# Constants and weights loaded inside the first attention's own programs, first batch first

## The reference

```
q_in  = x + pos_enc ;  kv_in = ctx + pos_enc
q     = layer_norm(q_in) @ Wq ;  k, v = layer_norm(kv_in) @ Wk, Wv
y     = layer_norm(q_in) + softmax(q k^T / sqrt(8)) v @ Wo
y     = y + gelu(layer_norm(y) @ W1 + b1) @ W2 + b2
```

## Time and profile before

| | us |
|---|---|
| median of 3 runs | 2394.16 (2392.81 to 2394.26) |
| profiled execution, its own time | 2392.34 |
| its span in the trace | 2390.6 |
| PE busy | 2199.2 (92%) |
| DVE busy | 1464.7 (61%) |
| ACT busy | 1314.9 (55%) |
| POOL busy | 697.8 (29%) |

### The profile page before, as it was taken

One profiled execution on the slowest core, in us unless ns is written; L12 is line 12 of the kernel. 1 busy time (PEld: TensorE's weight loads), 2 busy tenths in 40 slices (PEclk: granted clock), 3 DMA queues, 4 the chain that ended last, 5 costly groups with the idle time before them and its releaser, 6 DMA issues. The chain is left out here.

```text
span 2390.6 us, 49371 instructions
## 1 busy us (share of the span) xinstructions
PE 2199.2 (92%) x18720; PEld 1815.7 (76%) x18720; DVE 1464.7 (61%) x2824; ACT 1314.9 (55%) x3809; POOL 697.8 (29%) x664
## 2 busy tenths in 40 slices
PE   5999978999878799999999999999998889999979
PEld 3666646877767688888888888888886776776668
DVE  4788743444463566666666666666666337999953
ACT  3777743454543454444445544444444439999953
POOL 4443302101170533020111503030101406677740
PEclk9999988999989899999999999999999899999989
DMA  3000001000010101010100001010000210000000
GB/s 123 20 15 11 2 1 54 2 2 2 2 36 22 61 17 45 1 36 10 30 16 10 28 19 36 3 34 1 1 1 36 71 50 7 2 2 2 2 9 28
DMA packets 33671, 50.70 MB, mean 21 GB/s; under 512 B 2592, under 2 KB 22048, under 8 KB 32416
## 3 DMA queue, kind: packets, MB, share of 16 engines
q1 hardware_dynamic: 33440, 47.53, 6.4%
HBM read 45.43 MB, written 2.10 MB: 20 GB/s over the span
## 5 line engine op out<-in xcount | busy, mean ns | idle before, releaser
L605 ACT ACTIVATE l_probs<-l_s_psum,l_neg_max 128x129 f32<-128x129 f32 x512 | 181.5, 367 | 266.6 <-DVE l_neg_max L656 266.6
L678 DVE TENSOR_TENSOR x<-x,l_o_psum 128x512 f32<-128x512 f32 x256 | 176.0, 688 | 187.7 <-PE l_o_psum L559 186.1
L2310 ACT ACTIVATE l_probs<-l_probs,l_neg_max 128x128 f32<-128x128 f32 x512 | 210.7, 531 | 0.0
L445 POOL TENSOR_TENSOR l_head_w_high<-l_head_raw,one 128x768 fp32r<-128x768 f32 x32 | 47.2, 1476 | 516.1 <-PE l_o_psum L559 516.0
L590 ACT ACTIVATE l_KT<-l_k_psum,cols 128x512 f32<-128x512 f32 x128 | 88.2, 689 | 198.5 <-PE l_k_psum L122 198.5
L1159 DVE TENSOR_REDUCE l_neg_max<-l_psum 128x2 f32<-128x512 f32 x256 | 164.7, 683 | 47.6 <-PE l_psum L955 47.5
L2141 POOL TENSOR_TENSOR l_probs<-l_probs,l_mask_add 128x512 f32<-128x512 f32 x128 | 162.1, 1288 | 85.1 <-DVE l_probs L2367 85.1
L559 PE MATMUL l_o_psum<-l_head_w_high,l_context_low 128*128 128x256 f32 x512 | 155.5, 304 | 8.6 <-DVE l_context_low L661 8.6
L1094 ACT ACTIVATE l_PT<-l_psum 128x512 f32<-128x512 f32 x256 | 132.1, 603 | 55.3 <-PE l_psum L983 52.7
L661 DVE SCALAR_TENSOR_TENSOR l_context_low<-l_c_psum,cols,l_context_high 128x512 fp32r<-128x512 f32 x128 | 95.8, 749 | 106.2 <-ACT l_context_high L597 105.4
L1666 DVE TENSOR_REDUCE l_neg_max<-l_psum 128x2 f32<-128x512 f32 x128 | 84.7, 687 | 117.7 <-PE l_psum L1480 117.7
(11 more groups left out here) (279 smaller groups left out, 6650.0 us busy)
## 6 DMA issues: line engine op xcount, KB each, us to landing
l_head_raw<-in_l_heads SPq DMA_DIRECT2D x32, 384.0 KB, 3.0
l_w<-in_l_w SPq DMA_DIRECT2D x4, 1024.0 KB, 8.4
l_ctx_in<-in_ctx_T SPq DMA_DIRECT2D x16, 256.0 KB, 5.3
l_value_raw<-in_l_values SPq DMA_DIRECT2D x8, 512.0 KB, 3.5
l_value_rows<-in_l_rows SPq DMA_DIRECT2D x8, 512.0 KB, 5.1
l_x_in<-in_x_T SPq DMA_DIRECT2D x16, 128.0 KB, 2.2
l_x_in<-in_ctx_T SPq DMA_DIRECT2D x16, 128.0 KB, 2.5
values<-in_l_w SPq DMA_DIRECT2D x2, 1024.0 KB, 5.9
```

The lines of the kernel that those rows point to most:

```text
L605: last = act.activation(probs[:, i, :], scores[:, i // 2, i % 2, :], ACT.Exp, bias=neg_max[:, i:i + 1], scale=1.0, accum_out=den[:, i:i + 1])
L678: dve.tensor_tensor(out=x, in0=x, in1=o_bank[:, :], op=ALU.add).then_inc(o_free, 1)
L2310: last = act.activation(p, p, ACT.Exp, bias=neg_max[:, s % SCORES3, m:m + 1], scale=1.0, accum_out=den[:, u % 2, 4 * r + m:4 * r + m + 1])
```

## The change

`load_constants` and its Block are gone. Its memsets, selects and the cast become `make_constants`, called at the head of POOL's program in `attention0`. The DMAs move into SP's program there, in a new order: load(0), pos, shapes, cols, load(1), the four attention weights, load(2), load(3), the two feed-forward weights, rows, layer 1's six weights, then load(4) and on; at its end SP waits for the feed-forward weights and rows. Each group has a semaphore of its own. POOL waits for shapes and then for pos ahead of place(0), ACT waits for cols, PE waits for the constants and the attention weights. The memsets of neg_parts and V move from POOL to DVE; ACT no longer waits for them.

```diff
-def load_constants(c):
-
-    nc = c.nc
-    loaded, made, shapes_loaded = (c.lasting(n) for n in ("constants_loaded", "constants_made", "shapes_loaded"))
-    with nc.Block() as block:
-
-        @block.sync
-        def _(sync):
-            sync.dma_start(c.shapes[:, :], c.dram["shapes"]).then_inc(shapes_loaded, 16)
-            sync.dma_start(c.cols[:, :], c.dram["cols"]).then_inc(loaded, 16)
-            sync.dma_start(c.rows[:, :], c.dram["rows"].rearrange("(a n) -> a n", a=1).to_broadcast([P, N_ROWS]))\
-                .then_inc(loaded, 16)
-            mine = [n for n in WEIGHTS_01 if n.startswith("l0")]
-            for name in mine:
-                sync.dma_start(c.w[name][:, :, :], c.dram[name]).then_inc(loaded, 16)
-            sync.dma_start(c.pos[:, :, :], c.dram["pos"]).then_inc(loaded, 16)
-            sync.wait_ge(loaded, 16 * (3 + len(mine)))
...
-            pool.wait_ge(made, 11)
+L0_ATTENTION = ("l0_wq", "l0_wk", "l0_wv", "l0_wo")
+
+
+def make_constants(pool, c):
+
+    pool.memset(c.ident[:, :], 0.0).then_inc(c.made, 1)
...
+    pool.wait_ge(c.shapes_loaded, 16)
+    pool.tensor_copy(c.select[:, :], c.shapes[:, 2 * H:3 * H + 8]).then_inc(c.made, 1)
...
-            for u in range(B):
+            load(0)
+            sync.dma_start(c.pos[:, :, :], c.dram["pos"]).then_inc(c.pos_loaded, 16)
+            sync.dma_start(c.shapes[:, :], c.dram["shapes"]).then_inc(c.shapes_loaded, 16)
+            sync.dma_start(c.cols[:, :], c.dram["cols"]).then_inc(c.cols_loaded, 16)
+            load(1)
+            load_weights(sync, c, L0_ATTENTION, c.l0_loaded)
+            load(2)
+            load(3)
+            load_weights(sync, c, ("l0_w1", "l0_w2"), c.rest_loaded)
+            sync.dma_start(c.rows[:, :], c.dram["rows"].rearrange("(a n) -> a n", a=1).to_broadcast([P, N_ROWS]))\
+                .then_inc(c.rest_loaded, 16)
+            load_weights(sync, c, LAYER1_WEIGHTS, c.l1_loaded)
+            for u in range(4, B):
                 load(u)
-                if u == 3:
-                    load_weights(sync, c, LAYER1_WEIGHTS, c.l1_loaded)
+            sync.wait_ge(c.rest_loaded, 16 * 3)
...
-            pool.memset(neg_parts[:, :, :], 0.0).then_inc(set_up, 1)
-            pool.memset(V[:, :, :, :, :], 0.0).then_inc(set_up, 1)
-            pool.wait_ge(set_up, 2)
-            pool.memset(V[:, :, :, :, 8:9], 1.0).then_inc(set_up, 1)
+            make_constants(pool, c)
+            pool.wait_ge(c.pos_loaded, 16)
...
         def _(pe):
+            pe.wait_ge(c.made, 11)
+            pe.wait_ge(c.l0_loaded, 16 * len(L0_ATTENTION))
             pe.wait_ge(set_up, 3)
...
         def _(act):
-            act.wait_ge(set_up, 3)
+            act.wait_ge(c.cols_loaded, 16)
...
         def _(dve):
+            dve.memset(neg_parts[:, :, :], 0.0).then_inc(set_up, 1)
+            dve.memset(V[:, :, :, :, :], 0.0).then_inc(set_up, 1)
+            dve.wait_ge(set_up, 2)
+            dve.memset(V[:, :, :, :, 8:9], 1.0).then_inc(set_up, 1)
             dve.wait_ge(set_up, 3)
```

More of the change, by code:

```diff
@@ new lines @@
+L0_ATTENTION = ("l0_wq", "l0_wk", "l0_wv", "l0_wo")
+def make_constants(pool, c):
+    pool.memset(c.ident[:, :], 0.0).then_inc(c.made, 1)
+    pool.memset(c.ident_bf[:, :], 0.0).then_inc(c.made, 1)
+    pool.memset(c.ones_bf[:, :], 1.0).then_inc(c.made, 1)
+    pool.memset(c.minus_half[:, :], -0.5).then_inc(c.made, 1)
+    pool.memset(c.epsilons[:, 0:1], 1e-5).then_inc(c.made, 1)
+    pool.memset(c.epsilons[:, 1:2], 1e-6).then_inc(c.made, 1)
+    pool.memset(c.quarter[:, :], 0.25).then_inc(c.made, 1)
+    pool.memset(c.one[:, :], 1.0).then_inc(c.made, 1)
+    pool.wait_ge(c.made, 8)
+    for m in (c.ident, c.ident_bf):
+        pool.affine_select(out=m[:, :], in_=m[:, :], compare_op=ALU.not_equal, fill=1.0, base=0,
+                           pattern=[[-1, P]], channel_multiplier=1).then_inc(c.made, 1)
+    pool.wait_ge(c.shapes_loaded, 16)
+    pool.tensor_copy(c.select[:, :], c.shapes[:, 2 * H:3 * H + 8]).then_inc(c.made, 1)
@@ L2471, in build @@
         c.lasting = lambda n: ctx.enter_context(nc.semaphore(n))
+        c.made, c.pos_loaded, c.shapes_loaded = (c.lasting(n) for n in ("constants_made", "pos_loaded", "shapes_loaded"))
+        c.cols_loaded, c.l0_loaded, c.rest_loaded = (c.lasting(n) for n in ("cols_loaded", "l0_loaded", "rest_loaded"))
         c.l1_loaded = c.lasting("l1_weights_loaded")
@@ L2507, in build @@
                         c.pos = pos
-                        load_constants(c)
                         attention0(c)
```

## The result

The changed kernel takes 2387.94 us (median of 13 runs, 2383.06 to 2391.86), the kernel before 2394.06 in the same series (13 runs, 2391.49 to 2403.72). The ratio estimated from all these runs is 0.9971, with a 95% interval of 0.9961 to 0.9981: 6.9 us faster, between 4.5 and 9.3 (the two medians alone differ by 6.1). A second series gave 0.9976 (0.9964 to 0.9988). The forecast was 2384.0 with 9.4 us of gain; the median lies in the range of 2380.5 to 2388.5, close to its upper end, and the gain is about three quarters of the forecast.

The account below looks back on a forecast made before the run. PE was busy 92% of the span, so the gain had to come from the start-up chain ahead of its first matmul: 9.4 us earlier, all later terms nothing. Forecast 2384.0 us, between 2382.9 and 2384.8; range 2380.5 to 2388.5.

Parts of the forecast that it names:

- place(0) and its three conditions: At start-up, place(0) needs x and context, pos, and shapes with its cast; forecast at 5.1 us (4.6 to 7.3), before 14.47.
- 3.1 us for pos: At start-up, the transfer time assumed for pos with 256 KB ahead of it, landing it at 4.75 us.
- 543 KB by bytes: Start-up check: x, context, pos and shapes total 543 KB, there at 4.4 us, or 4.8 with completion.
- rival 1: At start-up, pos takes 5.4 us and place(0) begins at 7.3; gain 7.2, time 2386.9; chance 0.09.
- What is late next: Inputs after place(0): load(1) at most 0.3 us late; load(2), attention weights and others cost nothing.
- load(4): At place(4) on POOL: lands at 26.6 us, 2.8 late, but round(1) at 32.2 leaves 4.3 us; price nothing.
- Rival 3: At place(4) on POOL, load(4) lands after 30.9 us (237 GB/s), stalling the pipeline; 2394.6 us at 165 GB/s; chance 0.04.
- DVE's new memsets: At DVE's start: memsets end at 3.0 us, or 5.3 at double price, before DVE is wanted at 6.4; cost nothing.
- `attention0` and each later stage then end 9.4 earlier with the same lengths.: From `attention0` to the end: the start-up lead of 9.4 us is kept through every stage.
- the prediction's own last sign: In the stages after start-up: the prediction is wrong if a later stage has another length than before.
- Rival 2: PE's clock rises later in some stretches, losing 2.6 to 5 us, time 2389 to 2391, or gives 2.6 back; chance 0.07.
- The sum: Whole kernel: 2392.34 less 9.4 gives 2382.9, the median less 9.4 gives 2384.8; 2384.0 taken between.

Follow-up runs that it names:

- b3: The changed kernel with two more transfers of 1024 KB queued behind layer 1's weights and ahead of load(4); ratio 0.9958 (0.9943 to 0.9973).
- c2: The kernel before with only the memsets of neg_parts and V moved from POOL to DVE; ratio 1.0012 (1.0003 to 1.0021).
- a4: The changed kernel with POOL's round waiting, from batch 2 on, for DVE's subtraction of the batch before; 2385.23 us, ratio 0.9971 (0.9960 to 0.9983).
- c3: The changed kernel with eight more one-column memsets at the start of DVE's program; ratio 0.9968 (0.9958 to 0.9977).
- a3: The kernel before with POOL's round waiting, from batch 2 on, for DVE's subtraction of the batch before; ratio 1.0002 (0.9993 to 1.0011).
- b2: The changed kernel with a Block and its barrier kept for POOL's fills, without DMAs; ratio 0.9969 (0.9956 to 0.9981).
- b1: The changed kernel with the transfers in the old order, so only the barrier is gone; ratio 0.9998 (0.9985 to 1.0012).
- b4: a4 with ACT's table load moved ahead of its wait for cols; 2383.92 us, ratio 0.9952 (0.9933 to 0.9970).
- c4: b4 with the wait of POOL's round from batch 1 on instead of batch 2; 2384.36 us, ratio 0.9954 (0.9941 to 0.9968).
- c1: The changed kernel with the memsets of neg_parts and V back on POOL, behind the constants; ratio 0.9971 (0.9962 to 0.9981).

## Why the prediction was right, and where it was off

- **place(0) and its three conditions.** Forecast 5.1, measured 5.20, and shapes came last as said. The 3.1 us for pos and the 543 KB by bytes were good prices. That pos could take the 5.4 of its old row was rival 1; it didn't happen in any of the kernels with the new order.
- **What is late next.** load(1) was 0.29 us late at POOL, and root(0) began 2.77 after place(0) in place of 2.73. The attention weights and cols waited for nobody. PE began at 13.11 (forecast 12.9).
- **load(4).** Forecast 26.6 and round(1) at 32.2 released by ACT with 4.3 us left; measured 26.11, 31.50 and 4.11. The flat rate of 282 GB/s was luck in part: in the changed kernel the stream moved 203 to 238 GB/s from 4 to 10 us and 421 to 438 from 16 to 22, and only the mean from 4 us to the landing, 6.37 MB in 22.1 us or 288 GB/s, is about the one assumed. That everything issued ahead lands ahead, which the count of bytes takes for granted, agrees with the kernel before: the first 64 KB weight, issued at 2.10 after the 1408 KB of rows at 1.63, took 6.3 us and landed at 8.4, rows at 8.1.

```profile
rows<-in_rows SPq DMA_DIRECT2D x1, 1408.0 KB, 6.5
```

  load(4) was issued at 13.49 and not at 12.8, since SP's issue of wo took 1.37 us in place of 0.43; it landed 12 us later, behind what the queue held, so this cost nothing. Its decisive point is where the sum put it (place(4) near 31), by b3. Rival 3 needed 237 GB/s or less and didn't happen.
- **"DVE's new memsets ... Nothing."** This is the step that failed. As work they are hidden, as the sum said: they end at 3.4 and DVE is wanted at 6.6. But each instruction added at the head of DVE's program moves all later ones, and with them the place where an instruction is issued 0.17 us late. In this kernel that place fell on a pair where DVE and POOL start within 0.01 us. The price read from the trace is 1.0 us for each of two lost races. c2 has the move of the memsets alone, with one race lost, and is slower than before by 2.9 us (0.7 to 5.0).
- **"`attention0` and each later stage then end 9.4 earlier with the same lengths."** By the prediction's own last sign this is a miss: the body of `attention0` is 2.8 us longer (245.2 against 242.4), 3.4 in the second profile. Two of these are the races. The bodies of the eight traces without a lost race differ by 0.9 among themselves (241.5 to 242.4). The rest goes with a fall of the granted clock ahead of the stage's end: in the stretch 320 to 324 us of the changed kernel it reads 0.79, where the kernel before has 1.00.

```profile
320.00:324.00 4.00, 2.21 (x26) 1.07 (x26) 0.00 (x0) 2.34 (x5) 0.00 (x0) 0.79 0.00 0
```

  This fall, of 3 us, is in five of the six traces with a lost race and in none of the eight without. Why it goes with the races stays open.
- **Rival 2, the clock.** The form was right and the size too small in one place. I priced the stretches after `attention0` (0.9 us each). The larger effect is in the first batches: with the rise of the clock within 2 us of exp0, exp0 to nT0 takes 52.0 to 52.1 us; 5 or more later it takes 53.2 to 56.0. It can be worth 4 us, and it differs between runs of one kernel. From nT15 to the end the 14 traces have 2045.8 to 2052.6 us, and show no relation to the change. The three runs at hand, within 1.5 us, made me think too little of it: the 13 of the kernel before in the result lie within 12.
- **The sum.** In the two profiled executions: 9.3 at the start, 0.8 more in the first batches through the clock, less 2.8 in the body, gives 7.3 at nT15; 1.0 more goes in the stages behind, whose lengths differ as much between runs of one kernel, and 6.3 are left in the span. The ratio gives 6.9. The mechanism of the start-up was right, and the term that was missing in the traces is the 2 us of the races, with what goes along with them. The times of the runs don't resolve that term: a4 and c3, without a lost race, gain 6.9 us (4.1 to 9.6) and 7.7 (5.5 to 10.1), the changed kernel 6.9 (4.5 to 9.3). What else keeps the runs below 9.4 stays open.
- **The range.** That the median lies in it is luck in part. Its upper end was put there for a late place(0) (rival 1), which didn't happen; the median is 0.6 us inside it, and six of the 13 runs lie above it.

## What to carry to other kernels

A start-up chain can be priced from the timeline to some tenths of a microsecond: order of issue, time per issue, bytes ahead in the queue, and what each engine waits for last; most of the lead at place(0) came from the order of the transfers (7.5 us) and little from the barrier (1.8). A steady pipeline in which VectorE and GpSimd are released at the same moment and one blocks the other, as here, is fragile: an edit far away, on an idle engine, cost a microsecond per collision in this trace, so it is worth looking for ties, and a wait that orders the pair was free here (a3: ratio 1.0002). Where runs scatter by 3 us and more, compare lengths between the same two instructions in the traces, and keep the stretches at another clock apart.

## What the runs showed of the hardware

**A late issue at a fixed place of a program.** With DVE's program as in the changed kernel, the subtraction of batch 9 is issued 0.39 us after the cast and elsewhere 0.22. With two instructions more (b2) the delay comes ahead of the cast, whose idle time reads 0.58 in place of 0.23; with eight more (c3) it is off the pair. In the 2 us from 196 on the DMA view of the changed kernel has one packet of kind "instruction" on queue 14. It moves with the late instruction: in all nine traces in which one of the pair is late at batch 9, such a packet starts 0.66 to 0.69 us after the start of the late subtraction, or 0.57 to 0.59 after that of the late cast, and in c3 it starts 3.1 us ahead of the cast. That the delay has to do with the fetch of DVE's instructions is likely from this; no run shows that the fetch causes it. The Trainium skill, page "Advanced Engine Details and Errata", section "ISA Cache", says that instructions are cached in large lines, of which an engine holds only two; a delay at a fixed place would fit, and no run here measures the cache.

**The second lost race has another cause.** At batch 12 the subtraction isn't late after the cast (0.22), the cast itself comes 0.03 us later than in other batches, and 0.03 is enough. In b1 it is less still: the subtraction starts 0.006 us after the round and is blocked, while in batches in which it starts up to 0.004 after the round it isn't. The delay is there in a4, b4 and c4 too, whose wait keeps it from costing a race. The lost race is gone with DVE's old program (c1), with eight more instructions (c3) and in both kernels with a Block ahead (b2, c2). What makes the 0.03 wasn't found.

**PE's clock at the start.** In the changed kernel's first profile the granted clock is 0.50 from 22 to 39 us, that is 1.2 GHz, after it had been 1.00 for 3 us:

```profile
22.00:24.00 2.00, 1.99 (x10) 1.59 (x8) 2.00 (x5) 2.00 (x6) 2.00 (x2) 0.50 1.03 325
36.00:38.00 2.00, 2.00 (x25) 1.42 (x18) 0.04 (x1) 0.44 (x1) 2.00 (x2) 0.50 0.03 8
...
40.00:42.00 2.00, 1.31 (x32) 0.89 (x24) 1.46 (x4) 1.45 (x4) 0.00 (x0) 1.00 0.00 0
```

Where the clock has not yet changed in a trace this column reads 1.00, though the durations are those of 1.2 GHz, as in the earlier trace rows; it can't be trusted ahead of the first change. In this run, with the early 3 us at 2.4 GHz, round(1) comes at 31.50 and not at 32.46 as in the second profile, which has no such stretch; that accounts for the 0.8 us by which the lead exceeded the start-up's. In the unchanged kernel before, the rise came at 49.2 in one run and at 57.0 (after an earlier, short one) in the other. The same work thus meets another clock in each run. The Trainium skill, page "TensorE: Matmul & The Clock Gate", Part 1, says that the window in which activity is watched doesn't start with the kernel, and these runs agree.
